# ScalarE copies a chunk's transposed attention output before the logarithm and exponential of the square sums, in the steps that open a chunk

## What is computed

```python
qkv = shift_token(x) @ wqkv                 # 8 heads of 64
q, k = l2norm(q) * qs, l2norm(k) * ksc
q, k = rotary_xpos(q, k)
o = local_attention(q, k, v)                # windows of 64, each sees itself and the one before
x = x + o @ wo
h = layer_norm(shift_token(x)) * lg + lb
a, g = split(h @ w1 + b1)
x = x + (a * gelu(g)) @ w2 + b2
```

## Time and profile before

| what | value |
|---|---|
| time, median of 3 runs | 1206.1 us |
| the three runs | 1204.74, 1206.1, 1282.53 us |
| span of the profiled execution | 1203.1 us |
| instructions in it | 25908 |
| busy: PE, PEld | 1023.2 us (85%), 634.0 us (53%) |
| busy: DVE, ACT, POOL | 720.7 us (60%), 687.8 us (57%), 524.8 us (44%) |

### The profile page before, as it was taken

One profiled execution on the slowest core, in us unless ns is written; L12 is line 12 of the kernel. 1 busy time (PEld: TensorE's weight loads), 2 busy tenths in 40 slices (PEclk: granted clock), 3 DMA queues, 4 the chain that ended last, 5 costly groups with the idle time before them and its releaser, 6 DMA issues.

```text
span 1203.1 us, 25908 instructions
## 1 busy us (share of the span) xinstructions
PE 1023.2 (85%) x9070; PEld 634.0 (53%) x9070; DVE 720.7 (60%) x1625; ACT 687.8 (57%) x1301; POOL 524.8 (44%) x405
## 2 busy tenths in 40 slices
PE   3789999999998876799999999999729978755995
PEld 1345555555555354355555555555319964324995
DVE  0568677777766653577677676777654422555441
ACT  2566675685583562676575576564516646723661
POOL 2655456545532532544434444441354540253451
PEclk9889999999999977999999999999859989856998
DMA  9895434444434600544434434341412230011223
GB/s 345 253 285 163 94 84 107 97 117 107 105 77 97 70 2 2 124 107 107 106 82 109 97 95 101 89 107 42 166 49 60 66 103 23 18 35 48 65 66 121
DMA packets 88511, 120.02 MB, mean 100 GB/s; under 512 B 20064, under 2 KB 72032, under 8 KB 87488
## 3 DMA queue, kind: packets, MB, share of 16 engines
q1 hardware_dynamic: 81824, 96.30, 33.4%
q0 software_dynamic: 6272, 20.44, 4.6%
q10 hardware_dynamic: 288, 1.63, 0.3%
HBM read 62.66 MB, written 22.11 MB: 70 GB/s over the span
## 4 chain that ended last, share of the span: by engine, by line
PE 61%; ACT 16%; issue 9%; DVE 6%; DMA 4%; POOL 2%; SPq 1%; DVEq 0%; ACTq 0%; POOLq 0%
PE banks L942 6%; PE banks L952 6%; PE banks L591 6%; PE banks L662 5%; PE banks L676 5%; PE banks L751 3%; PE banks L620 3%; PE banks L637 3%; ACT arena L1187 3%; PE banks L669 3%; PE banks L721 2%; POOL moe_rows L2009 2%; PE banks L726 2%; DMA arena<-arena 2%; ACT arena L1197 2%
## 5 line engine op out<-in xcount | busy, mean ns | idle before, releaser
L2037 POOL TENSOR_TENSOR arena<-arena 128x1024 f32<-128x1024 f32 x64 | 150.8, 2356 | 338.0 <-DVE arena L1640 334.3
L2026 POOL TENSOR_TENSOR arena<-arena 128x1024 f32<-128x1024 f32 x64 | 150.7, 2355 | 42.1 <-ACT arena L1187 42.1
L1179 ACT ACTIVATE arena<-banks,arena 128x512 f32<-128x512 f32 x128 | 80.5, 679 | 95.1 <-PE banks L669 94.7
L591 PE MATMUL banks<-arena 128*128 128x512 f32 x256 | 126.4, 618 | 6.7 <-DVE arena L1559 5.9
L1632 DVE TENSOR_REDUCE arena<-banks 128x4 f32<-128x512 f32 x128 | 82.5, 686 | 80.9 <-PE banks L620 80.1
L2016 POOL DMA_INDIRECT moe_outs<-arena x78 | 82.1, 1053 | 99.5 <-DVE arena L1878 91.4
L1382 ACT ACTIVATE arena<-banks,arena 128x128 f32<-128x128 f32 x312 | 89.0, 369 | 58.4 <-PE banks L942 58.1
L2009 POOL DMA_INDIRECT moe_rows<-arena x64 | 63.3, 990 | 118.6 <-DVE arena L1613 101.0
L1640 DVE TENSOR_TENSOR arena<-arena 128x1024 f32<-128x1024 f32 x64 | 78.1, 1220 | 28.0 <-DMA arena<-arena 28.0
L952 PE MATMUL banks<-arena 128*128 x624 | 87.4, 284 | 4.5 <-ACT arena L1382 3.8
L1192 ACT ACTIVATE arena<-banks 128x1024 f32<-128x1024 f32 x64 | 65.6, 1025 | 44.4 <-PE banks L591 43.5
(11 more groups left out here) (221 smaller groups left out, 1931.6 us busy)
## 6 DMA issues: line engine op xcount, KB each, us to landing
arena<-arena SPq DMA_DIRECT2D x256, 128.0 KB, 3.8
arena<-rstd SPq DMA_DIRECT2D x128, 256.0 KB, 4.2
moe_rows<-arena POOLq DMA_DIRECT2D x12, 903.0 KB, 6.2
arena<-moe_rows SPq DMA_DIRECT2D x78, 64.5 KB
arena<-in_rot SPq DMA_DIRECT2D x4, 1024.0 KB, 11.4
arena<-in_mw SPq DMA_DIRECT2D x2, 2048.0 KB, 10.9
arena<-moe_outs SPq DMA_DIRECT2D x16, 256.0 KB, 4.7
arena<-ssm_a SPq DMA_DIRECT2D x4, 512.0 KB, 5.9
```

Source lines behind the costliest of these rows:

```text
L591: mm(bank[k], w_qkv[d][:, w0:w0 + P], src, start=True, stop=True).then_inc(proj, 1)
L2026: nc.gpsimd.tensor_tensor(TA[:, n % 2], RAW, ROTV[:, :, 0, c * C:(c + 1) * C], ALU.mult).then_inc(cos_done, 1)
L2037: nc.gpsimd.tensor_tensor(TA[:, n % 2], TA[:, n % 2], TB, ALU.add).then_inc(rot_sum, 1)
```

## The change

In the opening steps s = 8, 12, 16, 20, 24 and 28 of each run of F, `evacuate_out(s - 4, n - 4)` is called between `copy_out` and `inverse_norm` and no longer behind `inverse_norm`. All other steps keep their order, step 32 with them. No instruction is added or taken away.

```diff
                     if s < STEPS:
                         square(n)
                         copy_out(s, n)
+                        if hp == 0 and g >= 2:
+                            evacuate_out(s - 4, n - 4)
                         inverse_norm(n)
                     elif run:
                         act.wait_ge(ss_mm, n)
@@
-                    if s >= 4:
+                    if s >= 4 and not (hp == 0 and g >= 2 and s < STEPS):
                         evacuate_out(s - 4, n - 4)
```

## The result

| | before | changed |
|---|---|---|
| median of 6 runs | 1210.01 us | 1196.63 us |
| lowest, highest | 1204.74, 1282.53 us | 1192.29, 1202.75 us |
| span of the profiled execution | 1203.1 us | 1193.0 us |

The ratio of the changed kernel to the one before is 0.9918, with a 95% interval of [0.9891, 0.9945]: 9.9 us less on the median of before. It is less than 2%, so the verdict is "same", with a gain that is clear of its interval. The ratio leaves out the slow run of 1282.53 us. The two medians of the table are further apart, by 13.4 us. Measured later beside other kernels the ratio was 0.9883 [0.983, 0.9936].

What follows compares the result with a forecast made beforehand. The prediction took PE, busy 85% of the span, to bound the kernel, with waits at L683 for ACT's copy. 12 x 0.85 = 10.2 us off the 1206.1 median gave 1195.9 us, range 1192 to 1202.

Steps and rivals of the forecast that it cites:

- 11.2: Upper bound of the gain in us: the copy's whole delay, 0.93 us in each of the 12 opening steps.
- The place and the number of waits: At L683, PE idles for the copy L1197 12 times, 0.81 us each, 9.7 us in all.
- How soon L683 could start: In opening steps L683 could start 1.03 us behind L620, as in step 32, gaining 0.88 us.
- margin for the copy's semaphore: At L683 the copy's semaphore reaches PE at 193.29, 0.08 us before PE could start at 193.37.
- half hidden: Rival at L683: PE waits again after a 0.4 us lag, gain 5.4 us, time 1200.7 us; chance 0.09.
- 0.85 a step: L690 and what follows come 0.85 us earlier in each of 12 opening steps, 10.2 us in all.
- The logarithm and exponential at no cost: On ACT both start 0.48 us later, within 0.43 us of slack at L1226 and later consumers; cost 0.
- 1.2 us of cover on SyncE: SP issues swaps until L460 at 195.32, so the exponential ending at 194.11 is still 1.2 us early.
- second cover: L466 on SP waits until 201.62 for DVE's unit_done, covering a late L460; without cover, 5.8 us lost.
- The slack of 0.7 us for the swaps: In the closest step, swaps land by 244.3, before the next L1187 at 244.99; other eleven over 1 us.
- The rule against it: Skill rule, applied to PE's waits at L683: weight-load share 53% leaves room, so the gain could fall to nothing.

Runs made afterwards that it cites:

- first-run kernel: Against the kernel before, the copy moved only in the six opening steps of F's first run; median 1209.46 us, ratio to before 0.9963.
- half-way case: Against the kernel before, the copy put between logarithm and exponential in the opening steps; median 1209.26 us, ratio to before 0.9967.
- longer copy: Changed kernel plus an extra 128x1024 copy behind the moved one in opening steps; median 1202.19 us, ratio to before 0.9948.
- late exponential: Changed kernel with opening steps' exponential behind L1226 and an extra 128x512 copy ahead of it; median 1198.31 us, ratio to before 0.9905.

## Why the prediction was right

The forecast was 1195.9 us in a range of 1192 to 1202, and the median was 1196.63. The span was forecast at 1192.9 and is 1193.0. The medians of before were not the same (1206.1 in what was shown, 1210.01 over six runs), so the ratio is the better test: 10.2 of 1206.1 is 0.9915, measured 0.9918, and 0.9883 the second time. That the median agreed to 0.7 us and the span to 0.1 is partly luck. The same sum taken from 1210.01 would have given 1199.8, and the stretches outside F differ by 0.5 to 1.2 us with either sign between the two profiles. What is shown beyond luck is the 0.84 us of each opening step. The lower end of the range, 1192, is the span less 11.2; from the fastest run, which the prediction names, it would be 1193.5.

- *The place and the number of waits.* 12 waits of 0.81, all gone. Shown by the view of L683, and by the first-run kernel, which kept six.
- *How soon L683 could start.* 1.03 behind L620, taken from step 32; measured 1.04. The margin for the copy's semaphore held in all 12 steps, but it was thinner than the 0.08 us of the prediction. In its new place the copy took 0.61 us and not 0.58, and L683 starts 0.17 us behind its end, where it had started 0.14 behind it while waiting. The copy ahead of `copy_out`, 1.1 us earlier, gained nothing more. So neither "half hidden" nor a remainder came up. The half-way case was made on purpose, and there too L683 starts 0.14 us behind the copy's end (592.56 to 592.70), so the lag of the semaphore was reckoned rightly.
- *0.85 a step.* Measured 0.84 to 0.86 in the distances. The two L1187 that were to stand 43.94 apart stand 43.95 apart (199.32 and 243.27). The working had 0.03 us less for L690 than for L683, and so it is: 1.91 from one to the other.
- *The logarithm and exponential at no cost.* Right, and by what was named: 0.43 of slack at L1226 was predicted and is in the profile; the longer copy shows that this is where the limit is. The 1.2 us of cover on SyncE and the wait of L466 behind it were shown by the late exponential. The prediction put the point at which SyncE is through with its swaps at 195.2, 2.45 us behind the first of them; the late exponential, at 3.30, passed it by 0.85 us and cost nothing, as the second cover said.
- *The slack of 0.7 us for the swaps.* Not used up by the change, nor by half a microsecond more in the kernel with the copy ahead of `copy_out`. But the prediction took the wrong step for the closest, and the other eleven do not all have over 1 us. In step 8 of the first run, in the kernel before, the swaps took longer to land:

```profile
L450 SPq DMA_DIRECT2D arena<-arena x4: 567/582/591, 104.5 to 106.4; - x4
DMA to landing us min/median/max: 4.1/4.2/4.4
```

  Read as the prediction read its own step, they are there by 106.4 + 4.4 = 110.8, and the next L1187, at 112.11, less 0.85 stands at 111.26: 0.5 us. The landing itself, 110.52, leaves 0.7, and in the changed kernel it was 0.88. The conclusion held, with less room than the prediction claimed for that step. In steps 4 and 5 of the first run, on which the prediction said nothing, `copy_out` waits for swaps.
- *The rule against it.* The Trainium skill (Perfetto Trace Analysis, Identifying the Most-Contended Engine) has TensorE's headroom judged by MFU, the matmul work done as a share of the peak, and by the busy share of its weight loads, and not by that of its matmuls. That a wait taken from TensorE therefore need not come back was the prediction's own conclusion; the page says nothing of a single wait. It did not hold for F: all of the waits came back as time. In 44 us of the changed kernel's second run of F TensorE's matmuls, by their modelled ends, leave 0.5 us free, while its weight loads take 23.8:

```profile
552.00:596.00 44.00, 43.48 (x411) 23.78 (x408) 32.10 (x57) 28.87 (x46) 20.09 (x13) 1.00 0.45 101
```

The columns are the stretch, its length, busy us of TensorE, of its weight loads, of VectorE, ScalarE and GpSimd, granted clock, DMA share and GB/s. The distance of starts between neighbouring groups, which rests on no modelled end, is what decided it.

## What to carry to other kernels

Look for a copy that frees a bank for an engine that is waiting, and that stands in its own engine's order behind instructions whose result has a later consumer. Moved ahead of them it gained here the other engine's wait at that place, once for each time it occurs, up to that engine's own next work. A step of the same loop that lacks the instructions in between showed that limit to 0.01 us. Where runs scatter by more than the gain, the distance between equal points of the loop, from start to start, tells what a median can't.

## What the runs showed of the hardware

TensorE's clock was behind a part of the time in steps 4 and 5 that the expectation had not counted. In the kernel before, TensorE waits 2.38 us at L546 in step 4 of the first run. In the seven microseconds from 62 on the granted clock was then 0.57 and 0.50 of full on average, at or near the lower of its two levels (1.2 of 2.4 GHz). The windows, with the columns as above:

```profile
62.00:66.00 4.00, 2.52 (x12) 1.02 (x14) 2.48 (x5) 1.80 (x5) 3.92 (x2) 0.57 1.04 311
66.00:69.00 3.00, 3.00 (x17) 1.74 (x14) 0.83 (x3) 0.53 (x2) 2.04 (x4) 0.50 1.04 279
```

With the copy ahead in step 4 the wait is 1.31 us and the clock stays at the upper level. The same windows of that kernel:

```profile
62.00:66.00 4.00, 3.31 (x26) 1.91 (x27) 3.22 (x8) 2.38 (x5) 3.97 (x2) 1.00 1.01 276
66.00:69.00 3.00, 2.54 (x12) 1.24 (x10) 1.38 (x2) 2.92 (x5) 2.03 (x4) 1.00 1.09 241
```

Two matmuls of 512 columns took 2.08 us at the lower level and 1.10 at the upper. In the changed kernel, whose wait in that step is 2.31 us, L550 took 2.08 us too. So between these two profiles a wait 1 us shorter came with about 1 us less of slow matmuls behind it.

In these profiles it goes with the length of the wait and not with the edit. The kernel with the longer extra copy has the changed kernel's code in steps 4 and 5. In its profile the wait in step 4 happened to be 1.66 us, the clock stayed at the upper level, and L550 (L552 there) took 1.10 us:

```profile
62.00:66.00 4.00, 3.11 (x24) 1.72 (x25) 2.55 (x7) 1.50 (x4) 4.00 (x3) 1.00 1.03 268
66.00:69.00 3.00, 2.54 (x12) 1.26 (x11) 1.38 (x2) 2.91 (x5) 1.30 (x3) 1.00 1.08 255
```

Of the thirteen profiles, the eight with waits of 2.19 to 2.46 us there have slow matmuls at L546 or L550, or at both, and the five with 1.66 us or less have none. How much of this goes to the wait and how much to the rest of that stretch was not tried.
